# Loading x first and counting, gathering and splitting later in a two-layer graph kernel

## The chip, the cores and the metric

The kernel runs on one core of a Trainium2 chip. The metric is the device time of one execution in microseconds (us). Engines: PE is TensorE, DVE is VectorE, ACT is ScalarE, POOL is GpSimd, SP is SyncE, which here only issues DMAs. ACT issues some as well.

## The reference, cut to what matters

Two layers over 3125 nodes of 256 features and 100000 edges. Each has a graph part, a mixing part and a feed-forward part with experts.

```python
xn = layernorm(x)                                  # x: [3125, 256], no learned scale
neigh = segment_sum(xn[src], dst)                  # 100000 edges, sorted by dst
h = relu(((1 + eps) * xn + neigh) @ W1 + b1) @ W2 + b2
gnn = batchnorm(h)
q, k, v = split(rmsnorm(xn, g_pre) @ w_qkv)        # 4 heads of 32, plus 4 memory keys
q = softmax(q over features) * scale; k = softmax(k over nodes)
mix = rmsnorm((q @ (k.T @ v)) @ w_out + b_out, g_out) + xn
x = x + gnn + mix
x = x + experts0(layernorm(x))                     # top 2 of 8, relu
xn = layernorm(x)
x = x + two_graph_convolutions(xn, edge_weight) + mix1(xn)
xn = layernorm(x)
x = x + gelu(xn @ W1s + b1s) @ W2s + b2s + experts1(xn)   # shared part, and top 2 of 8
```


## The kernel before

X holds 25 tiles of 128 nodes. `first_norm_*` goes over 7 groups of 4 tiles (the last has one). For each, DVE takes statistics (`statistics_dve`) and a variance, ACT the root, DVE the reciprocal and bias, ACT writes the normalised rows XN, PE turns them (`turn_pe`, 8 transposes), ACT and DVE copy a half each to XT (`turn_act`, `turn_dve`), PE makes the q, k, v products of 4 tiles (`first_products_pe`), and ACT evacuates them with a scale (`first_products_act`), two groups behind. A tile's product waits for the evacuation four tiles earlier.

The edges are put to use through windows of two destination nodes. To find where each window begins, the first destination of each of 784 rows of 128 edges (`firsts`) is compared with each window (13 columns of windows: 7 counts on DVE in `windows_dve`, 6 sums of signs on ACT in `windows_act`). With the row numbers GpSimd gathers 13 rows of destinations (`windows_pool`, L306); DVE counts in these (`begins_dve`, L297) and gets where records start; GpSimd gathers 13 lots of records (dst, src, weight; L310). `places_dve` (L331), `places_act`, `places_in_tiles_dve`, `tiles_dve` and `keys_dve` turn records to keys, `good_dve` checks on a total of PE (`total_pe`) that all edges are inside, and `weights_dve` (L318) makes the degrees.

Before, `loads_act` issues the constants, `firsts` and x in three DMAs on ACT's queue, and `early_sp` nine small weights on SP's. All counts stand ahead of the first group. The row gathers run while the groups are normalised; `begins_dve` stands in group 4, and the record gathers follow at once. `mix0_*` is the attention: DVE takes maxima of q and k, subtracts, ACT takes exponentials, PE the context; `q_norm_dve` normalises q; cwo (L949) is the context times w_out; then for 7 groups PE turns q and multiplies, ACT takes squares (L868) and roots (L871), DVE scales (L957 to L967) and adds to X. The order on each engine is written out by hand and kept by semaphores.

SP then stores XN, zero pads (`zero_sp`), loads the late weights (`late_sp`), and stores the mix.

The end of layer 1: `conv_pe` finishes; the last group of 4 tiles is added and normed (`last_*`), while the shared feed-forward part runs over 13 tiles of 256 nodes. `between` orders it: `tile(i)` is the first product of tile i (48 matmuls, L1947), `second(i - 1)` the second product of the tile before (48, L1962), with two steps of routing between (`route_*`; 17 steps on DVE give the slot numbers). A weight is used as a high and a low part: `parts_act` copies the high, `parts_dve` subtracts (L1858). `halves_dve` (L1863, L1865) does so for the input of a tile, `first_dve` (L1886, L1888) for its hidden values. `warm_pe` are small matmuls without use of their result.

PE's order there is: first product of tile 0, 8 warm matmuls, first product of tile 1, the last group's turn, second product of tile 0, scores. ACT does the last group's root ahead of the copy of the second weights and of tile 1; DVE does scales and `parts_dve` ahead of `halves_dve` of tile 1.

## Time and profile before

| | us |
|---|---|
| median of 3 runs | 2214.99 (2212.96 to 2215.39) |
| profiled execution | 2201.3 |
| its span | 2199.7 |
| PE busy | 2063.6 (94%) |
| DVE busy | 1648.3 (75%) |
| ACT busy | 1241.5 (56%) |
| POOL busy | 594.7 (27%) |

The profile's page divides the span in 40 slices of 55 us. PE's busy tenths there start with 5, 7, 6, 9, then are 9 nearly throughout; DVE's start with 6, 9, 9, 8. The clock that the throttle granted to PE is 7 tenths in the third slice, 8 in the twelfth and the last, and 9 in all others. A time in the rows below is counted from the start of the span. A row of the view in order of time may merge several instructions (x4), and then its duration is from the first's start to the last's end.

### The profile page before, as it was taken

The numbers are of one execution on the slowest core, as the hardware profiler recorded it, in microseconds if no ns is written. First come the engines' busy times: TensorE is split into PE (matmuls) and PEld (weight loads), VectorE is DVE, ScalarE is ACT, GpSimd is POOL, SyncE is SP. The second block draws the span as 40 slices with busy tenths as digits, with TensorE's granted clock in tenths as the row PEclk, the third lists the DMA queues.
The fourth block names the chain that finished last, engine by engine and source line by source line (L and its number), as shares of the span: only waits on it lengthen the run. The fifth ranks groups of instructions, "written<-read, shape, count | busy, mean of one in ns | idle before, by whom it ended". The sixth has DMA issues, their size and how long they took to land. (4 is left out here: it accounts for less than half of the span.)

```text
span 2199.7 us, 46493 instructions
## 1 busy us (share of the span) xinstructions
PE 2063.6 (94%) x17860; PEld 1938.7 (88%) x17860; DVE 1648.3 (75%) x3103; ACT 1241.5 (56%) x2885; POOL 594.7 (27%) x462
## 2 busy tenths in 40 slices
PE   5769999999889999998999999999998999999996
PEld 3559999999689999997788999999998999999996
DVE  6998888885688888875657666566656868888885
ACT  6866555554547676665543444444444236767765
POOL 3100000000047777760000000000000016677774
PEclk9979999999989999999999999999999999999998
DMA  4424333344458778774004666466641026787776
GB/s 133 139 91 122 92 105 108 92 116 139 159 173 221 232 223 246 219 232 105 1 26 113 189 188 188 115 179 182 192 147 61 20 95 215 215 243 221 240 223 165
DMA packets 241142, 338.98 MB, mean 154 GB/s; under 512 B 33439, under 2 KB 202578, under 8 KB 240786
## 3 DMA queue, kind: packets, MB, share of 16 engines
q1 hardware_dynamic: 208940, 296.19, 42.5%
q0 software_dynamic: 28528, 35.76, 8.6%
q10 hardware_dynamic: 3446, 3.97, 0.6%
q8 instruction: 146, 2.39, 0.4%
q14 instruction: 82, 0.67, 0.1%
HBM read 258.89 MB, written 76.95 MB: 153 GB/s over the span
## 5 line engine op out<-in xcount | busy, mean ns | idle before, releaser
L2484 PE MATMUL bank<-WB_r,XN_r 128*128 128x448 f32 x1400 | 400.4, 367 | 0.4 <-DVE X L2261 0.4
L2017 POOL DMA_INDIRECT SC<-xd,slot_i x128 | 182.7, 1428 | 791.3 <-DVE slot_q L1653 659.8
L2419 ACT CAST WB_r<-WB 128x448 fp32r<-128x448 f32 x350 | 198.0, 567 | 248.0 <-PE bank L2484 229.3
L2424 DVE TENSOR_TENSOR WB_r<-WB,WB_r 128x448 fp32r<-128x448 f32 x350 | 217.2, 632 | 155.4 <-ACT WB_r L2419 155.0
L2484 PEld LDWEIGHTS bank<-WB_r,XN_r 128*128 128x128 f32 x1400 | 261.2, 188 | 22.6 <-DVE X L2261 0.8
L1947 PE MATMUL bank<-SC_r,WB_r 128*128 128x256 f32 (+1 forms) x2064 | 253.0, 282 | 13.2 <-issue 10.9
L1947 PEld LDWEIGHTS bank<-SC_r,WB_r 128*128 128x128 f32 x2064 | 246.3, 190 | 17.8 <-issue 17.4
L1067 ACT CAST WB_r<-bank 128x200 fp32r<-128x200 f32 x391 | 144.4, 369 | 158.9 <-PE bank L1050 158.2
L1962 PE MATMUL bank<-R_r,H_r 128*128 128x256 f32 x1752 | 215.4, 282 | 5.0 <-DVE R_r L1858 5.0
L1962 PEld LDWEIGHTS bank<-R_r,H_r 128*128 128x128 f32 x1752 | 209.1, 189 | 5.4 <-issue 5.4
L2411 POOL TENSOR_TENSOR WB<-WB,CB 128x128 f32<-128x128 f32 (+1 forms) x56 | 27.3, 488 | 610.9 <-DMA WB<-adjw 609.9
L1947 PE MATMUL bank<-SC_r,XN_r 128*128 128x256 f32 x1392 | 169.4, 280 | 4.2 <-issue 2.9
L1947 PEld LDWEIGHTS bank<-SC_r,XN_r 128*128 128x128 f32 x1392 | 164.6, 188 | 8.1 <-issue 7.7
L1819 ACT ACTIVATE yo<-yo,slot_p 128x256 f32<-128x256 f32 x118 | 53.6, 502 | 208.4 <-DVE yo L1897 203.9
L1810 ACT ACTIVATE wb_<-bank,WB 128x256 f32<-128x256 f32 (+1 forms) x344 | 133.2, 477 | 66.7 <-PE bank L1947 39.1
L2023 POOL DMA_INDIRECT slot_p<-pd,slot_q x128 | 158.8, 1240 | 41.3 <-issue 32.6
L1107 PE MATMUL bank<-H_r,WB_r 128*128 128x256 f32 x625 | 164.9, 299 | 0.0
L2484 PE MATMUL bank<-WB_r,R_r 128*128 128x448 f32 x448 | 164.4, 367 | 0.0
L1107 PE MATMUL bank<-XN_r,WB_r 128*128 128x256 f32 x625 | 153.9, 282 | 0.0
L1067 ACT COPY X<-bank 128x200 f32<-128x200 f32 x391 | 148.5, 380 | 0.0
L1023 DVE TENSOR_TENSOR SC<-R,DR 128x1024 bf16<-128x1024 bf16 x196 | 134.0, 684 | 0.0
L1107 PEld LDWEIGHTS bank<-XN_r,WB_r 128*128 128x128 f32 x625 | 118.7, 190 | 0.1
(480 smaller groups left out, 5118.7 us busy)
## 6 DMA issues: line engine op xcount, KB each, us to landing
WB<-adjw SPq DMA_DIRECT2D x350, 224.0 KB, 2.8
WB<-in_f_pack SPq DMA_DIRECT2D x127, 512.0 KB
WB<-in_f_pack SPq DMA_DIRECT2D x62, 640.0 KB
adjw<-X SPq DMA_DIRECT2D x24, 1600.0 KB, 7.8
WB<-in_f_pack SPq DMA_DIRECT2D x65, 516.0 KB
xd<-XN SPq DMA_DIRECT2D x10, 640.0 KB, 6.7
y<-X SPq DMA_DIRECT2D x10, 640.0 KB, 3.3
X<-y SPq DMA_DIRECT2D x6, 640.0 KB, 7.1
```

The costliest lines, as they stand in the source:

```text
L1023: e.tensor_tensor(by_two(hot_lo[s][:, 0:m, :]), row(iota16, o), along(lo2, o, 128), ALU.is_equal).then_inc(S("lo1"), 1)
L1067: e.copy(to[b % 2][:, :, 8 * j:8 * j + 8].rearrange("p h (q r) -> p q h r", r=2), bank[:, :, i]).then_inc(S(name), 1)
L1107: m = e.matmul(bk[:, 0:D], CNT[b % 2][:, h, :], x[:, h * D:(h + 1) * D], start=(h == 0 and x is xnh), stop=(h == T - 1 and x is xnl), skip ...
L1810: m = e.activation(st[:, q * w:(q + 1) * w], B[hp][:, q * TS:q * TS + w], gfun[L], bias=b[:, hc:hc + 1])
L1819: e.activation(ob[:, q, :], ob[:, q, :], ACT.Copy, scale=slot_p[:, 2 * i + q:2 * i + q + 1]).then_inc(S("obs"), 1)
L1947: m = e.matmul(B[hp][:, q * TS:q * TS + w], p[:, c * HID + hc * 128:c * HID + (hc + 1) * 128], x[:, c * w:(c + 1) * w], start=(c == 0 and ...
L1962: m = e.matmul(bk[:, s * D:(s + 1) * D], x[:, hc * w + s * 128:hc * w + (s + 1) * 128], p[:, hc * D:(hc + 1) * D], start=(hc == 0 and n == ...
L2017: e.indirect_dma_start(yin[i % 2][:, q * D:(q + 1) * D], None, XD, bass.IndirectOffsetOnAxis(ap=slot_i[:, 2 * i + q:2 * i + q + 1], axis=0 ...
L2023: e.indirect_dma_start(slot_p[:, 2 * i + q:2 * i + q + 1], None, PD.rearrange("(r k) -> r k", k=1), bass.IndirectOffsetOnAxis(ap=slot_q[:, ...
L2419: e.copy(split_w(m)[0], RAW[m % PR]).then_inc(S("whigh"), 1)
L2424: e.tensor_tensor(al, RAW[m % PR], ah.bitcast(F32), ALU.subtract).then_inc(S("wlow"), 1)
L2484: mm_ = e.matmul(conv_bank(k, band, c)[:, 0:PW], x[st][:, o], y, start=(st == 0 and i == 0), stop=(st == T - 1 and i == 2))
```

## The change

Loads: SP issues all but the constants, in this order: x tiles 0 to 3, six of the small weights, tiles 4 to 7, tiles 8 to 11, `firsts`, tiles 12 to 23, three weights, the last tile. Groups 0, 1, 2 and 3 wait for their own.

Counts: the cast of `firsts` and the 7 counts of DVE stand in groups 1 to 4 (2, 2, 2, 1), the 6 of ACT in groups 1 to 3 (3, 2, 1), with the row numbers at the end of group 4. `begins_dve` stands behind the last group. GpSimd gathers records only when all first products are made. SP stores XN only when the records are in. Buffers move: `firsts` and its cast to R1, the counts' output to H.

PE makes group 0's products ahead of group 1's turn. In the mix, the places stand on DVE behind all three normalisations of q, then context, shift, low keys, tiles, check, cwo, keys; on ACT behind all of x's sums; on PE behind the context's product.

Shared tiles: PE warms 14 times, the last group's turn stands behind the second product of tile 0, the scores behind that of tile 1; routing steps begin at tile 2; DVE splits the next tile's input straight behind a tile, ahead of the second weights; ACT copies the second weights in tile 0 and does the last group's root and rows behind tile 1.

The diff, with unchanged lines mostly left out:

```diff
 SHT = 13
-W_IN = 16 * 9
+W_IN = 16 * 6
...
     wide_wb = nc.alloc_sbuf_tensor_at("wide_wb", [128, 12000], F32, offset=at["WB"])
-    firsts = WB[:, 0:784].bitcast(I32)
-    firstf = WB[:, 784:1568]
-    below = WB[:, 1568:1568 + WG * 392].bitcast(BF16).rearrange("p (g n) -> p g n", g=WG)
+    firsts = r1_all[:, 1856:2640].bitcast(I32)
+    firstf = r1_all[:, 2640:3424]
+    below = h_all[:, 0:WG * 392].bitcast(BF16).rearrange("p (g n) -> p g n", g=WG)
...
     def loads_act(e):
         e.dma_start(CB[:, :], a["consts"]).then_inc(S("consts"), 16)
-        e.dma_start(firsts, a["first"].partition_broadcast(128)).then_inc(S("first"), 16)
-        for i in range(2):
-            e.dma_start(X[:, 12 * i:12 * i + 12, :],
-                        a["x"][12 * i * 128:12 * (i + 1) * 128, :].rearrange("(t p) d -> p t d", p=128)).then_inc(S(f"x_in{i}"), 16)
-        e.wait_ge(S("set"), 1)
-        e.dma_start(X[0:LAST, T - 1, :], a["x"][(T - 1) * 128:N, :]).then_inc(S("x_in1"), 16)
+
+    def x_tiles_sp(e, t0, t1, name):
+        e.dma_start(X[:, t0:t1, :], a["x"][t0 * 128:t1 * 128, :].rearrange("(t p) d -> p t d", p=128)).then_inc(S(name), 16)
...
     def early_sp(e):
+        x_tiles_sp(e, 0, 4, "x_in0")
...
         e.dma_start(cols[:, 0:16], a["cols"]).then_inc(S("w_in"), 16)
-        e.dma_start(wo0, a["m_wout"]).then_inc(S("w_in"), 16)
-        e.dma_start(bout0, a["m_bout"].partition_broadcast(128)).then_inc(S("w_in"), 16)
-        e.dma_start(gout0, a["m_gout"].partition_broadcast(128)).then_inc(S("w_in"), 16)
...
         e.dma_start(epsc, a["eps"].partition_broadcast(128)).then_inc(S("w_in"), 16)
+        x_tiles_sp(e, 4, 8, "x_re")
+        x_tiles_sp(e, 8, 12, "x_out1")
+        e.dma_start(firsts, a["first"].partition_broadcast(128)).then_inc(S("first"), 16)
+        x_tiles_sp(e, 12, 24, "x_in1")
+        e.dma_start(wo0, a["m_wout"]).then_inc(S("x_in1"), 16)
+        e.dma_start(bout0, a["m_bout"].partition_broadcast(128)).then_inc(S("x_in1"), 16)
+        e.dma_start(gout0, a["m_gout"].partition_broadcast(128)).then_inc(S("x_in1"), 16)
+        e.wait_ge(S("set"), 1)
+        e.dma_start(X[0:LAST, T - 1, :], a["x"][(T - 1) * 128:N, :]).then_inc(S("x_in1"), 16)
...
-    def windows_dve(e, c):
+    COUNTS_DVE = {1: range(0, 2), 2: range(2, 4), 3: range(4, 6), 4: range(6, COUNTED)}
+    COUNTS_ACT = {1: range(COUNTED, 10), 2: range(10, 12), 3: range(12, WG)}
+
+    def firsts_dve(e):
...
         e.wait_ge(S("set"), 5)
-        for g in range(COUNTED):
+
+    def counts_dve(e, c, gs):
+        for g in gs:
             c.add(e.tensor_scalar(below[:, g, :], firstf, w2h[:, g:g + 1], None, ALU.is_lt, ALU.add, accum_out=cnt4[:, g:g + 1]))
+
+    def windows_dve(e, c):
...
         c.add(e.tensor_scalar(row4[:, 0:COUNTED], cnt4[:, 0:COUNTED], 1.0, 0.0, ALU.subtract, ALU.max))
-        e.wait_ge(S("mix0_act"), M0A_PLACES)
+        e.wait_ge(S("mix0_act"), M0A_KEXP)
...
-    def windows_act(e):
-        e.wait_ge(S("consts"), 16)
+    def windows_act(e, gs):
         e.wait_ge(S("set"), 5)
-        for g in range(COUNTED, WG):
+        for g in gs:
...
         e.wait_ge(S("rows"), 2)
+        e.wait_ge(S("qk"), T)
...
+    def shift_dve(e, c):
+        c.add(e.tensor_scalar(whii.bitcast(I32), esrc, 7, None, ALU.logical_shift_right))
+
     def places_in_tiles_dve(e, c):
-        c.add(e.tensor_scalar(whii.bitcast(I32), esrc, 7, None, ALU.logical_shift_right))
...
         def ready(t):
             if t == 0 and k == 1:
-                e.wait_ge(S("x_re"), 80)
+                e.wait_ge(S("x_re"), 96)
...
     M0P_KMAX, M0P_KALL, M0P_CTX, M0P_MASKED, M0P_CWO = range(5)
-    M0A_PLACES, M0A_KEXP, M0A_MEM = WG - COUNTED, WG - COUNTED + 1, WG - COUNTED + 5
-    M0V_W, M0V_RS, M0V_GROW, M0V_REL, M0V_KMAX, M0V_DIAG, M0V_KSUB, M0V_MEM, M0V_MASKED, M0V_CTX, M0V_CWO = (
-        0, 2, 5, 6, 7, 8, 9, 13, 14, 15, 16)
+    M0A_KEXP, M0A_MEM, M0A_PLACES = WG - COUNTED, WG - COUNTED + 4, WG - COUNTED + 5
+    M0V_W, M0V_RS, M0V_GROW, M0V_KMAX, M0V_DIAG, M0V_KSUB, M0V_MEM, M0V_REL, M0V_MASKED, M0V_CTX, M0V_CWO = (
+        0, 2, 5, 6, 7, 8, 12, 13, 14, 15, 16)
...
                 e.wait_ge(S("set"), 4)
+            if g == 1:
+                e.wait_ge(S("x_re"), 16)
+            if g == 2:
+                e.wait_ge(S("x_out1"), 16)
             if g == 3:
-                e.wait_ge(S("x_in1"), 32)
+                e.wait_ge(S("x_in1"), 80)
...
             e.tensor_scalar(sd[:, 0, o], mv[:, o, 1], 1.0, 1e-5, ALU.mult, ALU.add).then_inc(S("var"), 1)
-            if g == 4:
-                begins_dve(e, c)
...
                 turn_dve(e, 0, g - 1)
+            if g == 1:
+                firsts_dve(e)
+            if g in COUNTS_DVE:
+                counts_dve(e, c, COUNTS_DVE[g])
+            if g == 4:
+                windows_dve(e, c)
...
         turn_dve(e, 0, G - 1)
+        begins_dve(e, c)
...
                 first_products_act(e, t)
+            if g in COUNTS_ACT:
+                windows_act(e, COUNTS_ACT[g])
...
     def first_norm_pe(e):
-        for g in range(G):
+        turn_pe(e, 0, 0)
+        first_products_pe(e, 0)
+        turn_pe(e, 0, 1)
+        for g in range(2, G):
             turn_pe(e, 0, g)
-            if g:
-                first_products_pe(e, g - 1)
+            first_products_pe(e, g - 1)
...
         warm_pe(e, 2, 24)
-        total_pe(e)
...
         m.then_inc(S("mix0_pe"), 1)
-        places_pe(e)
...
         e.matmul(B[1][:, 0:D], kb, wo0, start=True, stop=True).then_inc(S("mix0_pe"), 1)
+        places_pe(e)
+        total_pe(e)
...
     def mix0_act(e):
...
         q_exp_act(e, 0)
-        places_act(e)
...
         x_sum_act(e, range(8, T))
+        places_act(e)
...
     def mix0_dve(e, c):
-        places_dve(e, c)
...
         e.tensor_tensor(memkT[:, :], memkT[:, :], kb[0:4, :], ALU.subtract).then_inc(S("mix0_dve"), 1)
-        q_norm_dve(e, c, 0)
-        places_in_tiles_dve(e, c)
-        good_dve(e)
+        for i in range(3):
+            q_norm_dve(e, c, i)
+        places_dve(e, c)
...
         e.scalar_tensor_tensor(km, B[2][:, 0:128], k2[:, 1:2], mask32, ALU.mult, ALU.mult).then_inc(S("mix0_dve"), 1)
-        tiles_dve(e, c)
+        shift_dve(e, c)
...
         e.tensor_copy(kb, B[0][:, 0:128]).then_inc(S("mix0_dve"), 1)
+        places_in_tiles_dve(e, c)
+        tiles_dve(e, c)
+        good_dve(e)
+        e.wait_ge(S("mix0_pe"), M0P_CWO + 1)
+
+        e.scalar_tensor_tensor(cwo, B[1][:, 0:D], HEAD_SCALE, bout0, ALU.mult, ALU.add).then_inc(S("mix0_dve"), 1)
         keys_dve(e, c)
-        e.wait_ge(S("mix0_pe"), M0P_CWO + 1)
-
-        e.scalar_tensor_tensor(cwo, B[1][:, 0:D], HEAD_SCALE, bout0, ALU.mult, ALU.add).then_inc(S("mix0_dve"), 1)
-        q_norm_dve(e, c, 1)
-        q_norm_dve(e, c, 2)
...
             if j == 0 and b == 1:
-                e.wait_ge(S("x_out1"), 32)
+                e.wait_ge(S("x_out1"), 48)
...
             tile(i)
-            if i:
+            if i >= 2:
...
                 second(i - 1)
-            if i:
+            if i >= 2:
...
     def sp_program(e):
...
         e.wait_ge(S("qk"), T)
+        e.wait_ge(S("edges"), 16 * WG)
...
     def act_program(e):
         loads_act(e)
-        windows_act(e)
...
         def begin():
-            e.wait_ge(S("slots"), 3)
+            e.wait_ge(S("slots"), 4)
...
         def tile(i):
+            if i == 2:
+                last_turn_act(e, G - 1)
...
             if i == 0:
+                parts_act(e, 1, 1, SHARED)
+            if i == 1:
                 last_root_act(e, G - 1)
-                parts_act(e, 1, 1, SHARED)
...
                     last_rows_act(e, G - 1, j)
-            if i == 1:
-                last_turn_act(e, G - 1)
...
     def dve_program(e):
...
         sets_dve(e, c)
-        windows_dve(e, c)
...
         def tile(i):
+            if i == 2:
+                last_turn_dve(e, G - 1)
             first_dve(e, 1, NSLOT + i, shared_w(i))
+            if i + 1 < SHT:
+                halves_dve(e, shared_x(i + 1), NSLOT + i + 1, shared_w(i + 1))
             if i == 0:
-                last_scales_dve(e, G - 1)
...
             if i == 1:
-                last_turn_dve(e, G - 1)
-            if i + 1 < SHT:
-                halves_dve(e, shared_x(i + 1), NSLOT + i + 1, shared_w(i + 1))
+                last_scales_dve(e, G - 1)
...
         def tile(i):
...
             if i == 0:
-                warm_pe(e, 6, 8)
+                warm_pe(e, 6, 14)
+
+        def second(i):
             if i == 1:
-                last_turn_pe(e, G - 1)
-
-        def second(i):
+                e.wait_ge(S("xt0"), 4 * G)
...
             if i == 0:
+                last_turn_pe(e, G - 1)
+            if i == 1:
...
```

## Rows read from the trace of the kernel before

**Rows 1.** busy time in two stretches: start:end, length, busy us (instructions), clock, DMA

```profile
20.00:66.00 46.00, 42.00 (x150) 25.73 (x150) 35.88 (x156) 30.57 (x65) 26.09 (x26) 1.00 0.26 75
62.00:106.00 44.00, 28.68 (x178) 24.67 (x177) 40.94 (x111) 38.45 (x64) 0.22 (x1) 0.88 0.52 154
```

**Rows 2.** groups of instructions, 0 to 66 us: busy us, mean ns, idle

```profile
L745 ACT ACTIVATE XN<-X,small 128x256 f32<-128x256 f32 x25 | 13.0, 589 | 4.3 <-DVE small L708 4.3
...
L277 DVE TENSOR_SCALAR_CACHE_REDUCE WB<-WB,CB 128x784 bf16<-128x784 f32 x7 | 6.7, 1023 | 0.0
L291 ACT ACTIVATE WB<-WB,CB 128x784 bf16<-128x784 f32 x6 | 5.6, 935 | 0.0
```

**Rows 3.** VectorE in order of time: start, duration, line, operation, idle before

```profile
19.76 1.41 DVE L495 BATCH_NORM_STATS2 small<-X 128x6 f32<-128x256 f32 x4
...
22.83 0.20 DVE L708 SCALAR_TENSOR_TENSOR small<-small 128x4 f32<-128x4 f32 x1
...
38.77 0.34 DVE L297 TENSOR_SCALAR_CACHE_REDUCE DR<-R,CB 128x128 f32<-128x128 int32 x1
...
62.87 3.04 DVE L331 TENSOR_SCALAR H<-H,CB 128x128 f32<-128x128 int32 x13 [0.47 <-DMA H<-in_edges,small]
65.81 1.61 DVE L886 TENSOR_REDUCE small<-wide_wb 128x44 f32<-128x1408 f32 x1
```

**Rows 4.** busy time and GB/s over the first 9 us

```profile
0.00:5.00 5.00, 0.00 (x0) 0.00 (x0) 2.39 (x7) 0.00 (x0) 0.19 (x4) 1.00 0.54 172
5.00:9.00 4.00, 0.00 (x0) 0.00 (x0) 1.17 (x4) 0.00 (x0) 0.00 (x0) 1.00 0.83 257
```

**Rows 5.** TensorE in order of time, first products to the last

```profile
29.17 1.38 PE L775 MATMUL bank<-wb_,XT 128*128 128x384 f32 x2
...
47.85 0.81 PE L775 MATMUL bank<-wb_,XT 128*128 128x384 f32 x2
...
65.07 0.81 PE L776 MATMUL bank<-wb_,XT 128*128 128x384 f32 x2
```

**Rows 6.** GpSimd in order of time: row gathers, then a record gather

```profile
20.14 1.12 POOL L306 DMA_INDIRECT R<-in_dst,small  x1 [19.39 <-DVE small L285]
...
35.33 0.95 POOL L306 DMA_INDIRECT R<-in_dst,small  x1 [0.30 <-issue]
43.00 0.94 POOL L310 DMA_INDIRECT H<-in_edges,small  x1 [6.73 <-DVE small L301]
```

**Rows 7.** VectorE in order of time, 93 to 110 us

```profile
93.77 0.40 DVE L949 SCALAR_TENSOR_TENSOR yo<-bank,rows 128x256 f32<-128x256 f32 x1
...
105.60 0.16 DVE L957 TENSOR_SCALAR small<-small 128x4 f32<-128x4 f32 x1
...
109.80 0.17 DVE L957 TENSOR_SCALAR small<-small 128x4 f32<-128x4 f32 x1
```

**Rows 8.** ScalarE in order of time, 71 to 108 us

```profile
71.72 1.68 ACT L344 ACTIVATE SC<-R,ones 128x1664 f32<-128x1664 f32 x1
...
107.49 0.21 ACT L871 ACTIVATE small<-small 128x4 f32<-128x4 f32 x1
```

**Rows 9.** TensorE in order of time, first halves of shared tiles 0 and 1

```profile
1658.09 5.84 PE L1947 MATMUL bank<-SC_r,WB_r 128*128 128x256 f32 x48 [0.68 <-issue]
...
1670.82 8.00 PE L1947 MATMUL bank<-SC_r,WB_r 128*128 128x256 f32 x48 [5.10 <-issue]
```

**Rows 10.** busy time and clock over the first half of shared tile 1

```profile
1670.80:1678.70 7.90, 7.88 (x49) 7.90 (x50) 2.53 (x5) 3.81 (x7) 0.00 (x0) 0.70 0.20 67
```

**Rows 11.** VectorE in order of time, near 1666 and 1670 us

```profile
1665.69 0.69 DVE L1888 TENSOR_TENSOR H_r<-wb_,H_r 128x512 fp32r<-128x512 f32 x1
...
1670.03 0.69 DVE L1865 TENSOR_TENSOR SC_r<-XT,SC_r 128x512 fp32r<-128x512 f32 x1
```

**Rows 12.** ScalarE in order of time, near 1665 us

```profile
1664.83 1.28 ACT L2616 ACT_TABLE_LOAD   x1
```

**Rows 13.** GpSimd in order of time, the first gather of the last slots

```profile
1782.69 1.01 POOL L2017 DMA_INDIRECT SC<-xd,slot_i  x1 [145.91 <-DVE slot_q L1653]
```

2 lines of the change are left out of this document (1 added, 1 removed).

## The prediction

> **What bounds the kernel.** I read the busy time by stretch first, because the change touches two places only: the first 110 us and 40 us near 1660. Over 20 to 66 us TensorE is busy 42.0 of 46 us; over 62 to 106 us it is VectorE, 40.9 of 44 us [rows 1]. So the opening has three parts: a wait for x, a TensorE-bound norm with first products, and a VectorE-bound stretch that lasts beyond 106 us. From about 160 us TensorE is full, so what either part saves is still there at the end if nothing later stands at a fixed time. All sums are against the profiled execution (2201.3 us, span 2199.7); the runs' median is 2214.99. I carry the difference over unscaled.
>
> **Part 1, the start.** Before, VectorE counts first rows (7 counts, 6.7 us, so 0.95 each) and ScalarE 6 (5.6 us, 0.93 each) [rows 2] ahead of the first statistics at 19.76; the first group's bias is ready at 23.03, 3.27 us later [rows 3]. Now tiles 0 to 3 are first on SP. With the constants beside them that is 0.88 MB, and 0.86 MB had moved by 5.0 us [rows 4], so I put their landing at 5.3. The first group's scaling of the weights waits for six small loads behind; 1.3 MB, at 257 GB/s from there [rows 4], and small pieces that are issued until about 6 us give 7.7 (ends 7 and 9.5). Bias ready at 9.0: 14.0 us sooner.
>
> The counts aren't gone, only moved. Groups 1 to 4 now carry them: 2, 2, 2, 1 on VectorE with a cast of 0.57, and 3, 2, 1 on ScalarE. ScalarE's round without waits is 4 rows of XN (2.07), a root with its answer from VectorE (0.65), a copy (0.5) and 4 evacuations (2.1), some 5.3 us: 0.589 us for a row [rows 2], less 0.09 where they overlap, and an evacuation taken as long as a row, since both make one tile. TensorE's round is 6.2 us: products of group 0 start at 29.17, of group 3 at 47.85 [rows 5]. So 2.8 and 1.9 us of signs make ScalarE the longer one in groups 1 to 3, and the counts put VectorE's variances late too. Worked through group by group (variance ready, XN written, products start):
> group 0: 7.5, 11.1, 14.7; group 1: 11.2, 14.0, 22.0; group 2: 17.8, 20.6, 29.6; group 3: 25.7, 28.4, 35.8; group 4: 31.1, 34.6, 42.7.
> Group 0's products start 14.5 us sooner, group 3's 12.0, and the last product ends 11.1 us sooner (65.88 becomes 54.8). About 3.4 us of the head start goes back to idle TensorE between groups. The products of group 0 moved ahead of group 1's turn fill some of it; alone they give 0 to 0.6 us.
>
> **Part 2, row and record gathers.** The 13 row gathers are issued every 1.25 us, from 20.14 to 35.33 [rows 6], and the last lands some 2.4 us after its issue, since the counts on these rows could start at 38.77 [rows 3]. That cover was free: before, they ran beside the norm. Now the first can go only when group 4's count is done, 36.6 by the table above, so the last lands at 36.6 + 0.3 + 15.2 + 2.4 = 54.5. VectorE was through with the norm at 62.40, where it waited 0.47 us for the records [rows 3]; now at 62.4 - 11.1 = 51.3, and it stands 3.2 us. The begins take 4.0 us (38.77 to the record gather's start at 43.00, less 0.3 on the queue) and have moved from the norm, where VectorE had room, onto the path: until 58.5. What stood at 65.81, the second group's q maximum [rows 3], starts at 58.8: 7.0 us sooner, not 11.1.
> The new wait of GpSimd for the last product costs nothing, as 54.8 is before 58.5. Records take 62.87 - 43.00 = 19.9 us and are there at 78.5.
>
> **Part 3, VectorE from there to the mix.** From 65.81 to 105.60 [rows 7] it was 39.8 us, the weights at its end included. The same work stands there now in another order, plus the places (2.9 us, 62.87 to 65.81), which were ahead of it; the wait of 1.0 us for the context goes, since three normalisations now stand ahead of it. The records at 78.5 meet VectorE at about 82: no wait. 58.8 + 39.8 + 2.9 - 1.0 = 100.5, and 0.4 for waits on the total, which now comes after the places' turn on TensorE: 100.9, 4.7 us sooner. Next limit: ScalarE's second root ended at 107.70 [rows 8], 2.1 us ahead of VectorE's use at 109.80. Its chain hangs on the first outputs, which start after cwo; cwo (end 94.17 [rows 7]) comes at 58.8 + 28.4 (94.17 - 65.81) + 2.9 for the places + some 5 for two normalisations, now ahead of it (three operations each of at most the 1.61 us at 65.81, the last group's small) - 1.9 for the keys, now behind it - 1.0 = 92.2, and 92.6 with the total's wait. That is 1.6 us sooner, so the root ends at 106.1. VectorE takes it at 106.1 and not at 105.2: 3.7 us sooner. From here both shift together. **Front: -3.7 us**, ends -8 (no stand on rows, root in time) and +2 (weights at 9.5, groups 1 to 4 each 1 us later).
>
> SP stores XN only when the records are in, 78.5 and not 65.9, so its stores of XN, zero fills and late weights slide by 12.6 us. Behind them on SP stand the y stores, the first of which wants the third added pair, some 1.9 us behind 109.80, now 108. Between 65.9 and there SP had 46 us for work of some 8 MB, 27 us at 300 GB/s; it keeps 29. If that doesn't hold, the y stores come late by the rest (0 to 3 us), and the buffers that X's place is to serve with them. The x loads share one queue, constants on the other; group 3 waits for all loads, about 19 us, and comes at 24.
>
> **The Sign activations** now stand between roots. A Sign ran straight behind an Exp's square at 71.72 with no table load in between [rows 8], so it is in the Exp table; whether the sqrt table has it no row shows. I take it that it does. (The Trainium skill, "ScalarE: Activation LUTs", Table sets, says cheap functions are in every set as filler, and names relu, copy, identity and abs; Sign isn't in that list, so it leans my way without settling it.)
>
> **Part 4, the shared tiles.** TensorE's first half of tile 1 started at 1670.82 after 5.1 us of idleness and took 8.00 us; tile 0's took 5.84 [rows 9]. The granted clock over those 7.9 us is 0.70, that is partly the lower level of 1.2 GHz [rows 10]. It waited for the low halves of tile 1, at 1670.03 to 1670.72 on VectorE [rows 11], behind a root with its table load of 1.28 us [rows 12], scales and the second weights' split. Now the halves follow VectorE's split of tile 0, done at 1666.38 [rows 11], directly: 1666.38 + 1.1 = 1667.5. TensorE warms 14 instead of 8 times; 8 took 1.9 us (1663.8 to 1665.7), 14 last until 1663.8 + 3.4 = 1667.2, so the idle gap is 0.3 us and I take the full clock: 1667.5 + 5.84 = 1673.3, against 1678.8. That is 5.4 us. What is late next: the second weights' split ends at 1669.9, used at 1673.4; the root comes after ScalarE's tile 1, at 1674.2 + 1.28 + 0.2 = 1675.7; scales 1676.7; the four rows of XN 1678.9; second half of tile 0 on TensorE ends 1679.2, and the turn of the last group behind it finds them ready by 0.3 us. Halves of tile 2 are there at 1676.3, wanted at 1680. The scores move behind tile 1's second half. I count 0.3 us for a slip: **-5.1 us**, ends -2 and -6.
> Route steps begin a tile later and there are 17, so the slot numbers come in tile 10 and not in 9, 11 us later by tile and some 6 by time. GpSimd took them at 1782.69 [rows 13], needs 13 us for the first two slots' gathers, and TensorE turns the first gathered rows only behind tile 12. Two tiles and more of 11 us lie between; covered by 10 us. The new wait for 4 instead of 3 holds ScalarE's weight copy by 2 us, covered by the product beside it.
>
> **Sum**: -3.7 - 5.1 = -8.8: 2192.5 in a profiled execution like the one before, 2206.2 as median.
>
> **Rivals.**
> A, the front gives nothing (chance 0.20): the gathers and begins, once under the norm, are a chain; each us that group 4's count is later moves all of VectorE. With the weights at 9.5 and four rounds 1 us longer, -3.7 becomes 0 to +2, in sum -4: 2211. For it: VectorE is nearly fully busy behind [rows 1]. Against: 3.2 us of stand are in my sum already.
> B, the Sign is not in the sqrt table (0.10): three groups of signs, two loads each, 6 x 1.28 = 7.7 us on ScalarE, just where it is the longer one; -8.8 + 7.7 = -1.1: 2213.9. The row at 71.72 speaks for a filler.
> By the Trainium skill's "ScalarE: Activation LUTs", What ACT_TABLE_LOAD costs, a switch is 2.66 us with its drain, and B would be +7; the row at 1664.83 shows 1.28, so I price by the row.
> C, the slower side (0.06): TensorE's clock falls in the gaps that now stand between the norm's groups. Products at the lower level take twice 5.16 us a group; two groups lost, and the change is at zero (-8.8 + 10.3); with four, +20.6 less some 4 of gaps: +8, 2223. It decides from the third group. For it: the fall after the idleness at 1665.7 [rows 9, 10]. Against: my gaps are 1 to 3 us, and the stretch to 66 us held full clock [rows 1].
> D, the tile split gives only 2 us (0.10): the clock falls all the same, or the last turn waits for XN: 2209.3.
> E, the whole front in hand (0.04), -8: 2202.
>
> Forecast 0.50. A run here tells 0.2% (4.4 us) from no change. Faster: forecast, E, most of D and half of A: 0.68. Slower: C and a little of A and B: 0.08. Same: 0.24. The range for 8 in 10, with the unknown ends of both parts: 2201 to 2214.
>
> **What would show it.** First XN row near 9 us; products of groups 0, 3 at 14.7 and 35.8; last product near 54.8; no table load in groups 1 to 3; VectorE idle some 3 us before the begins, waiting on the row gather; second q maximum near 58.8; the second normalisation of the mix at 106; in the tail first half of tile 1 with an idle gap under 1 us and 5.84 us long. I am wrong if the second q maximum starts after 63, or if tile 1's first half still takes over 7 us.

## The result, and the profile after

| | us, median (lowest to highest) |
|---|---|
| before | 2214.99 (2212.96 to 2215.39), 3 runs; profiled execution 2201.3, span 2199.7 |
| after | 2199.28 (2197.66 to 2200.47), 3 runs; profiled execution 2199.28, span 2197.7 |
| ratio | 0.9935, 95% interval 0.9919 to 0.9951: 15.7 us less |

Forecast was 2206.2, range 2201 to 2214: the change gave 15.7 us where 8.8 were summed. The two profiled executions differ by only 2.0 us. Both numbers have to be explained.

The same two stretches as in [rows 1], in the kernel after (columns as there):

```profile
20.00:66.00 46.00, 35.28 (x132) 20.91 (x130) 33.65 (x113) 30.33 (x60) 17.26 (x17) 0.96 0.10 28
62.00:106.00 44.00, 27.43 (x159) 25.02 (x160) 41.85 (x111) 34.10 (x58) 15.70 (x15) 0.74 0.68 203
```

TensorE's work has moved ahead of 20 us. Behind 62 us VectorE is as full as before, and TensorE's granted clock is 0.74 instead of 0.88: it is at its lower level of 1.2 GHz for more of the stretch. VectorE in order of time, to be read against [rows 3] and [rows 7]:

```profile
6.12 1.41 DVE L508 BATCH_NORM_STATS2 small<-X 128x6 f32<-128x256 f32 x4 [0.94 <-DMA X<-in_x]
...
9.01 0.16 DVE L723 SCALAR_TENSOR_TENSOR small<-small 128x4 f32<-128x4 f32 x1
...
57.12 0.35 DVE L307 TENSOR_SCALAR_CACHE_REDUCE DR<-R,CB 128x128 f32<-128x128 int32 x1 [2.68 <-DMA R<-in_dst,small]
...
61.12 1.61 DVE L912 TENSOR_REDUCE small<-wide_wb 128x44 f32<-128x1408 f32 x1
...
94.55 0.40 DVE L976 SCALAR_TENSOR_TENSOR yo<-bank,rows 128x256 f32<-128x256 f32 x1
103.22 0.15 DVE L983 TENSOR_SCALAR small<-small 128x4 f32<-128x4 f32 x1
...
109.24 0.17 DVE L983 TENSOR_SCALAR small<-small 128x4 f32<-128x4 f32 x1 [1.75 <-ACT small L897]
```

The reader is to see how a lead melts. The first bias is 13.8 us sooner (9.01 against 22.83), the second maximum of q 4.7 us (61.12 against 65.81), the first group of the mix 2.4 us (103.22 against 105.60) and the second group 0.6 us (109.24 against 109.80), since VectorE waits there for ScalarE's second root. TensorE in order of time, the first products, the key turns and the shared tiles, against [rows 5] and [rows 9]:

```profile
14.70 1.62 PE L801 MATMUL bank<-wb_,XT 128*128 128x384 f32 x2 [2.04 <-ACT XT L563]
16.11 1.49 PE L802 MATMUL bank<-wb_,XT 128*128 128x384 f32 x2
17.39 1.16 PE L801 MATMUL bank<-wb_,XT 128*128 128x384 f32 x2
18.39 0.81 PE L802 MATMUL bank<-wb_,XT 128*128 128x384 f32 x2
...
37.24 0.81 PE L801 MATMUL bank<-wb_,XT 128*128 128x384 f32 x2
...
91.11 3.05 PE L392 MATMUL bank<-CB,H 128*128 128x128 f32 x13 [1.65 <-DVE H L363]
...
1659.95 5.84 PE L1973 MATMUL bank<-SC_r,WB_r 128*128 128x256 f32 x48 [0.87 <-issue]
...
1669.40 5.89 PE L1973 MATMUL bank<-SC_r,WB_r 128*128 128x256 f32 x48 [0.49 <-issue]
```

Tile 1's first half now starts 9.45 us behind tile 0's instead of 12.73 us, and takes 5.89 us instead of 8.00. ScalarE in order of time, the only table load of the norm, and two places at the norm's end:

```profile
1.50 1.28 ACT L764 ACT_TABLE_LOAD   x1 [1.50 <-PEq L2928]
...
14.50 0.95 ACT L301 ACTIVATE H<-R,CB 128x784 bf16<-128x784 f32 x1
...
17.93 0.21 ACT L764 ACTIVATE small<-small 128x8 f32<-128x8 f32 x1 [0.52 <-DVE small L715]
...
51.31 0.58 ACT L781 ACTIVATE wide_wb<-bank,small 128x384 f32<-128x384 f32 x1 [3.67 <-PE bank L802]
...
55.65 0.58 ACT L781 ACTIVATE wide_wb<-bank,small 128x384 f32<-128x384 f32 x1 [1.97 <-PE bank L802]
...
109.00 0.21 ACT L897 ACTIVATE small<-small 128x4 f32<-128x4 f32 x1
```

A Sign (L301) stands between two roots (L764) with no load. And ScalarE was idle for 3.67 us ahead of copying out a product. It is tile 18's (tiles counted from 0, copied in order), and TensorE's row for it, in order of time, ends at 47.35:

```profile
46.54 0.81 PE L802 MATMUL bank<-wb_,XT 128*128 128x384 f32 x2
```

It copied it at 51.31, 4.0 us later. The end of a TensorE row is modelled, so this alone does not say that the product was ready at 47.35. But the trace also records the time of each semaphore update, and TensorE's signal for tile 18, for which ScalarE waits, is there at 51.22, 3.9 us behind the row's end and 0.09 us ahead of the copy. In the profile of the kernel before each of these 25 signals comes within 0.02 us of its row's end. So ScalarE waited for a late signal of TensorE. Late signals of this kind turned out to be the key to most of the missing microseconds.

### The profile page after: what moved, and what is told of

It reads as the page before. It is cut to its first block and busy times, and to the rows that moved or that the text cites. A ratio compares the mean times of both kernels' runs of the same rounds, so it can differ in the third digit from the quotient of the medians.

```text
span 2197.7 us, 46520 instructions
## 1 busy us (share of the span) xinstructions
PE 2071.7 (94%) x17872; PEld 1945.1 (89%) x17872; DVE 1649.9 (75%) x3103; ACT 1240.1 (56%) x2884; POOL 593.8 (27%) x462
```

## Experiments

Five comparisons, each on one chip with its own runs of the kernel before:

| comparison, chip | before, median (lowest to highest), runs |
|---|---|
| 1, A | 2201.53 (2197.93 to 2206.02), 27 |
| 2, B | 2215.43 (2211.36 to 2217.31), 11 |
| 3, A | 2202.12 (2198.71 to 2208.10), 32 |
| 4, C | 2212.27 (2209.26 to 2215.98), 13 |
| 5, D | 2202.32 (2197.65 to 2204.82), 11 |

**The parts, on chip A.** `plain` is the kernel before unchanged, `both` the change whole, `shared_only` and `front_only` the two halves of the diff. The shared half is

```diff
         def tile(i):
+            if i == 2:
+                last_turn_dve(e, G - 1)
             first_dve(e, 1, NSLOT + i, shared_w(i))
+            if i + 1 < SHT:
+                halves_dve(e, shared_x(i + 1), NSLOT + i + 1, shared_w(i + 1))
             if i == 0:
-                last_scales_dve(e, G - 1)
                 parts_dve(e, 1, 1, SHARED)
             if i == 1:
-                last_turn_dve(e, G - 1)
-            if i + 1 < SHT:
-                halves_dve(e, shared_x(i + 1), NSLOT + i + 1, shared_w(i + 1))
+                last_scales_dve(e, G - 1)
...
             if i == 0:
-                warm_pe(e, 6, 8)
...
+                warm_pe(e, 6, 14)
```

with ScalarE's and TensorE's last turn, root and scores moved likewise and the routing steps beginning at tile 2; the front half is everything else.

> The kernel before, unchanged. The profiled execution of before took 2201.3 us and its three timed runs 2213 to 2215.4. Theory S (a spread between loads of one program, of the order of 14 us, that has nothing to do with the change): the timed runs of this copy differ from those of the kernel before, or its profile shows a time more than 5 us away from 2201. Theory R (the 15.7 us are the change's): copy and kernel before agree within 2 us in every round, and the profile of a slow execution shows 14 us more at places that the change touches.

> The changed kernel again. Prediction's sum: 8.8 us less than before. By the two profiles at hand (2201.3 and 2199.3) only 2 us less. By the timed runs 15.7 us less. Theory R: 13 to 18 us less again. Theory S: 3 to 9 us less, with a spread over the rounds as large as the difference.

> Before, with the shared tiles' part of the change alone. Both theories: 5.1 us less (the first half of tile 1 starts 3.3 us sooner and takes 5.84 instead of 8.00 us). If the timed result is over 8 us, the shared part carries something that the profile of the tiles doesn't show.

> Before, with everything of the change but the shared tiles' part. Prediction: 3.7 us less. By the profile of the changed kernel the second root of the mix is taken at 109.2 instead of 109.8 (0.6 us less), 3.7 us of stall near 47 us included. Theory R: 8 to 11 us less, since the shared tiles can give only 5. Theory S: 0 to 4 us less.

| | comparison 1: median, ratio | comparison 3 (again): median, ratio |
|---|---|---|
| plain | 2203.45, 1.0003 (0.9994 to 1.0012) | 2201.61, 0.9998 (0.9989 to 1.0007) |
| both | 2194.31, 0.9962 (0.9948 to 0.9976) | 2195.31, 0.9971 (0.9962 to 0.9981) |
| shared_only | 2196.95, 0.9975 (0.9966 to 0.9984) | 2196.84, 0.9980 (0.9971 to 0.9989) |
| front_only | 2200.68, 0.9991 (0.9982 to 1.0000) | 2200.65, 0.9997 (0.9987 to 1.0006) |

The ratios times 2202 us are: whole change 8.4 and 6.4 us, shared part 5.5 and 4.4, front 2.0 and 0.7. The front's two intervals end at 1.0000 and 1.0006, so on this chip its gain is hardly told from nothing. So on this chip the sum of 8.8 nearly holds, and I took the 15.7 us for three odd runs of the kernel before. Comparison 2 took that away: eleven more runs of it at 2215.43, beside variants of the changed kernel at 2195.6 to 2198.2. What was asked next:

> The kernel before, unchanged, as a kernel of its own with a profile, on whatever chip this comparison gets. So far it stood at 2201.5 (38 runs on one chip), at 2215.4 (11 runs on another, where variants of the changed kernel took 2195.6 to 2198.2) and at 2215.0 in the three first runs. Theory L (two levels of the kernel before, set by the chip): here all its runs lie at one of the two, 2198 to 2206 or 2211 to 2217, with none between; at the upper one its profile shows one place 12 to 15 us longer than in the recorded profile of 2201.3. Theory D (drift spread over the kernel): the profile has each stage longer by its share, 0.6%, with no such place.

> The change without its shared-tile part. At the lower level of the kernel before it was 1 to 2 us faster. If the kernel before is at its upper level here and theory F holds (what costs the 14 us is in the front: x's loads behind others on the queue, or the records), this kernel is at 2198 to 2203, 12 to 16 us under; if theory T holds (it is in the shared tiles or behind them), it is at 2211 to 2215. At the lower level: 2199 to 2202 either way, and nothing is told apart.

> The kernel before with the shared-tile part of the change alone. At the lower level of the kernel before it was 5.5 us faster. If the kernel before is at its upper level here: theory F has this kernel at 2208 to 2212 (its 5.5 us alone), theory T at 2194 to 2199 (5.5 and the 14 us). At the lower level: 2195 to 2198.

> The whole change again. Theory L says that it has no upper level: 2193 to 2200 on every chip, so 7 to 9 us under the kernel before where that is at its lower level and 15 to 19 us where it is at its upper one. If this kernel too has an upper level that it only hadn't met, it may show here at 2207 to 2210.

It got chip A again (table above): nothing told apart, but the parts repeated. Comparison 4 then got a chip on which the kernel before is slow:

> The kernel before, unchanged, with a profile. It stood at 2201.5 and 2202.1 in two comparisons on one chip (59 runs of the reference and 22 of this copy, 2198 to 2208), at 2215.4 in one on another chip (11 runs, 2211 to 2217), and at 2215.0 in the three first runs. If this comparison gets a chip of the upper level, this copy is at 2211 to 2217 and its profile says where: theory F (in the front) has the second maximum of q some 14 us past 66.5, or the second group of the mix some 14 us past 110.5; theory T (in the shared tiles or behind them) has the products of shared tile 0 at their old place and tile 3 past 1698 by 14; theory D (spread over all tiles) has tile 0 of the shared tiles some 10 us past 1658. On a chip of the lower level: 2198 to 2206, every mark within 2 us of these.

> The change without its shared-tile part. Upper level of the kernel before: theory F 2198 to 2203, theory T 2211 to 2215, theory D anywhere between and up to the level of before. Lower level: 2199 to 2202 (0 to 2 us under the kernel before), the second group of the mix near 110.

`plain3` 2212.26 (2207.08 to 2218.41, 10 runs), ratio 1.0000; profiled execution 2210.59. `front_only3` 2201.33 (2197.74 to 2204.02), ratio 0.9949 (0.9932 to 0.9966): the front alone gives 11.3 us there, against 0.7 to 2.0 on chip A. Theory F holds: the difference is in the front. Now VectorE, ScalarE and TensorE of `plain3` in order of time:

```profile
39.76 0.18 DVE L706 RECIPROCAL small<-small 128x4 f32<-128x4 f32 x1 [3.94 <-ACT small L742]
...
59.71 0.16 DVE L706 RECIPROCAL small<-small 128x1 f32<-128x1 f32 x1 [6.32 <-issue]
...
65.35 0.69 DVE L560 COPY XT<-bank 128x512 f32<-128x512 f32 x1 [3.53 <-remote]
...
74.99 1.61 DVE L886 TENSOR_REDUCE small<-wide_wb 128x44 f32<-128x1408 f32 x1
```

```profile
32.87 0.58 ACT L757 ACTIVATE wide_wb<-bank,small 128x384 f32<-128x384 f32 x1 [0.34 <-PE bank L776]
37.80 0.58 ACT L757 ACTIVATE wide_wb<-bank,small 128x384 f32<-128x384 f32 x1 [4.35 <-PE bank L776]
...
59.00 0.58 ACT L757 ACTIVATE wide_wb<-bank,small 128x384 f32<-128x384 f32 x1 [2.97 <-PE bank L776]
...
63.19 0.59 ACT L550 COPY XT<-bank 128x512 f32<-128x512 f32 x1 [2.49 <-PE bank L542]
```

```profile
32.86 0.81 PE L776 MATMUL bank<-wb_,XT 128*128 128x384 f32 x2
...
55.33 1.04 PE L542 MATMUL bank<-CB,XN 128*128 128x128 f32 x8
...
66.19 1.01 PE L775 MATMUL bank<-wb_,XT 128*128 128x384 f32 x2 [4.44 <-ACT wide_wb L757]
66.99 1.49 PE L776 MATMUL bank<-wb_,XT 128*128 128x384 f32 x2
68.27 1.49 PE L775 MATMUL bank<-wb_,XT 128*128 128x384 f32 x2
...
1667.22 5.91 PE L1947 MATMUL bank<-SC_r,WB_r 128*128 128x256 f32 x48 [0.94 <-issue]
```

and the same marks of `plain2`, the same program on chip A:

```profile
37.12 0.18 DVE L706 RECIPROCAL small<-small 128x4 f32<-128x4 f32 x1 [3.04 <-ACT small L742]
...
55.22 0.16 DVE L706 RECIPROCAL small<-small 128x1 f32<-128x1 f32 x1 [4.13 <-ACT small L742]
...
66.91 1.62 DVE L886 TENSOR_REDUCE small<-wide_wb 128x44 f32<-128x1408 f32 x1
```

ScalarE waits 4.35 us in group 0's products: TensorE's row for tile 1's ends at 33.67 (the pair of 32.86, 0.81 long), and the copy is at 37.80. It waits 2.97 us for group 3's last product, and 2.49 us for a turn. The semaphore updates in the trace say what it waited for:

| `plain3`, product of | end of TensorE's row | TensorE's signal | ScalarE's copy |
|---|---|---|---|
| tile 1 | 33.67 | 37.72 | 37.80 |
| tile 15 | 55.49 | 58.91 | 59.00 |
| tile 16 | 57.66 | 65.38 | 65.47 |
| tile 19 | 61.53 | 65.56 | 66.87 |

Every one of ScalarE's waits over 1 us for a product here ends within 0.1 us behind TensorE's signal, so ScalarE does not stand by itself: the signals come late, by up to 7.7 us. The four of tiles 16 to 19 come within 0.2 us of each other, while their rows lie 1.29 us apart. VectorE meets the same: its copy of a turn at 65.35 follows a signal at 65.32, and TensorE's row for that turn (55.33) ends at 56.37. Behind the late signals VectorE also waits for the root that ScalarE issues after the copies, and TensorE for banks, and after TensorE's idle 4.44 us its pairs take 1.49 instead of 0.81 us.

The second maximum of q comes at 74.99 against 65.81 in [rows 3]: 9.2 us, and the distance stays: the first half of shared tile 0 at 1667.22 against 1658.09 [rows 9] is 9.1 us, the span 2209.0 against 2199.7 is 9.3 us. So between these two executions nothing behind the norm differs by these marks. By the medians chip C is 10 us above chip A and chip B 13; the kernel before was not profiled on chip B, and what its rest is stays open. The four executions of the old front on chip A have no idleness over 1.01 us ahead of such a copy, the recorded profile of before none over 0.77, and in all five each signal comes within 0.02 us of its row's end: that is why no row shows it.

ScalarE and VectorE of `front_only3`, on the same chip C:

```profile
50.33 0.58 ACT L781 ACTIVATE wide_wb<-bank,small 128x384 f32<-128x384 f32 x1 [2.09 <-PE bank L802]
53.16 0.58 ACT L781 ACTIVATE wide_wb<-bank,small 128x384 f32<-128x384 f32 x1 [2.25 <-PE bank L802]
```

```profile
58.32 0.35 DVE L307 TENSOR_SCALAR_CACHE_REDUCE DR<-R,CB 128x128 f32<-128x128 int32 x1 [4.01 <-DMA R<-in_dst,small]
```

The waits are there too (2.09 and 2.25 us, where `both2` on chip A shows 0.40 and 0.71 on the same instructions), but VectorE waits 4.01 us for the row gathers anyway, as it does on chip A (4.00 us in `both2`). So the gather chain covers them. It is not the whole of it: ScalarE's waits over 0.9 us for TensorE behind 30 us add up to 14.1 us in `plain3`, 4.3 in `front_only3` and 5.6 in the kernel after, so the new front also meets less of them, and no run tells the two apart. Comparison 5 was to show this for the whole change:

> The whole change beside the kernel before on whatever chip this gets. Theory: the kernel before pays on some chips 7 to 9 us in the first norm, where ScalarE stands 3 to 4.4 us at a time with its product long done and the products stop behind it; in the changed kernel such stands lie beside VectorE's wait for the first rows' gathers. So on such a chip (before at 2210 to 2217): 2195 to 2200, ratio 0.992 to 0.995, stands of 2 to 4 us on ScalarE between 44 and 56, second maximum of q at 61 to 62.7 all the same. On the other kind (before at 2200 to 2203): 2193 to 2196, ratio 0.9955 to 0.9975, no stand of ScalarE over 1 us behind 44. If instead the changed kernel only happened not to meet them, it is at 2205 to 2210 on the first kind.

It got chip D, where the kernel before takes 2202: `both3` 2194.39 (2193.30 to 2196.09), ratio 0.9965 (0.9953 to 0.9978), 7.7 us less, with no such wait. So the whole change was not run beside the kernel before on a chip like B or C again; for those stand the recorded 15.7 us, the front's 11.3 us of comparison 4, and comparison 2 below.

**What bounds the changed front**, on chip B and without the changed kernel beside them:

`warm_start`, in first_norm_pe, around the first turn:

```diff
+        e.wait_ge(S("consts"), 16)
+        warm_pe(e, 7, 18)
...
+        warm_pe(e, 7, 8)
```

`counts_early`, the counts and, in first_norm_dve, behind the variance:

```diff
-    COUNTS_DVE = {1: range(0, 2), 2: range(2, 4), 3: range(4, 6), 4: range(6, COUNTED)}
+    COUNTS_DVE = {1: range(0, 2), 2: range(2, 4), 3: range(4, COUNTED)}
...
+            if g == 4:
+                windows_dve(e, c)
...
-            if g == 4:
-                windows_dve(e, c)
```

`warm_mix`, in mix0_pe, behind the context, the masked turn and the matmul with wo0; `all3` has all three edits:

```diff
+        warm_pe(e, 3, 16)
...
+        warm_pe(e, 3, 8)
...
+        warm_pe(e, 3, 10)
```

> The changed kernel with TensorE's idle front filled: 18 throw-away matmuls ahead of the norm's first turn and 8 behind it, in a bank that is free. In the profile of the changed kernel the first pairs of products took 1.62, 1.49 and 1.16 us, later ones 0.81. Theory 1 (clock at the start): the pairs take 0.81 from the first, group 0's products end 1.7 us sooner, and since groups 1 to 4 follow back to back the last product comes at 54.4 to 55.5 instead of 56 to 57; if the products set the rows and the rows set the begins, the time falls by 1.5 to 1.7 us against the changed kernel (2194.3 on this chip in the last comparison). Theory 2 (rows' chain): the begins wait for the row gathers and these for the counts on VectorE, which don't wait for TensorE, so the last product comes sooner but the second maximum of q stays at 61 to 62.7 and the time within 0.5 us.

> The changed kernel with the last counted windows taken in group 3 of the norm instead of group 4 and the window starts set right behind group 4's variance, ahead of its normalised rows' work. Theory 2 (rows' chain): rows are set some 3 us sooner (34 to 36 instead of 37.4 to 39), the first-row gathers land 3 us sooner, VectorE's wait of 2.7 to 4.0 us ahead of the begins shrinks to under 1, the second maximum of q comes at 58.5 to 60, and the records land 2 to 3 us sooner; the time falls by 1 to 3 us, less what group 4's products lose by the counts taken ahead of them. Theory 3 (clock and second root): what sets the mix is the context's turns and the second root, the sooner records only move the low keys; if TensorE falls to its lower level there again, the time falls by less than 1 us.

> The changed kernel with TensorE kept busy between the context and the key turns: 16 throw-away matmuls behind the context's, 8 behind the masked turn, 10 behind the one for the clip of weights. Before the change these turns took 1.75 us and the q turns 1.0; in the changed kernel 3.05 and 1.95 at the lower clock level, and the second root came 14.05 us behind the clip against 13.5. Theory 3 (clock and second root): the turns are back at 1.75 and 1.0, the second root comes 1.5 to 2.5 us sooner (106.5 to 107.5 instead of 109.0 by the recorded profile), the second group of the mix on VectorE at its first one's end (about 107.4 instead of 109.24), and the time falls by 1 to 2 us. Theory 2: the wait for the second root is covered by what follows, the mix's last group keeps its place, and the time stays within 0.5 us.

> The three edits together. If each theory holds for its own piece, the pieces add, since they lie one behind the other: 1.5 (start) + 1 to 3 (rows) + 1 to 2 (second root) = 3.5 to 6.5 us under the changed kernel, some 2188 to 2191 on a chip where that takes 2194.3. If only one of them sets the end, the gain is that one's alone, 1 to 2 us. It also shows again how the kernel before stands: near 2201 as in the 38 runs of the last comparison and its own profile, or at 2213 to 2215 as in the three first runs.

| | median, ratio to before on chip B | second q maximum | second group of the mix |
|---|---|---|---|
| warm_start | 2195.60, 0.9920 (0.9907 to 0.9933) | 59.73 | 108.63 |
| counts_early | 2198.23, 0.9921 (0.9909 to 0.9933) | 65.32 | 114.25 |
| warm_mix | 2197.32, 0.9922 (0.9909 to 0.9935) | 61.82 | 110.05 |
| all3 | 2197.41, 0.9922 (0.9910 to 0.9935) | 62.23 | 110.84 |

All four are 17 to 18 us under the kernel before by the ratios, and their runs overlap. `all3` was expected 3.5 to 6.5 us under the changed kernel, near 2190, and is no faster than the others. `counts_early` missed: its first row gather started at 36.05 instead of 37.67, but its second q maximum came 4.2 us later than in the kernel after. ScalarE of `counts_early` in order of time:

```profile
48.32 0.58 ACT L781 ACTIVATE wide_wb<-bank,small 128x384 f32<-128x384 f32 x1 [2.95 <-PE bank L802]
...
53.24 0.58 ACT L563 COPY XT<-bank 128x512 f32<-128x512 f32 x1 [3.22 <-remote]
```

Again the waits for late signals, now ahead of the last root and of the turn that the last products need. Here too a signal comes up to 8 us late (row's end 46.80, signal 54.75). TensorE idles 4.67 us and ends its products at 63.9 instead of 57.9, and VectorE starts the begins at 61.33 without a wait for the gathers. So the changed front is not safe from the late signals as such: in this order they are the limit again. In `warm_mix` the key turns take 1.66 us instead of 3.05, and the second root is no sooner (109.81): TensorE, then ScalarE, in order of time:

```profile
92.67 1.66 PE L392 MATMUL bank<-CB,H 128*128 128x128 f32 x13
```

```profile
93.33 2.95 ACT L419 CAST DR<-bank 128x1024 bf16<-128x1024 f32 x4 [1.29 <-PE bank L392]
96.14 1.12 ACT L889 COPY SC<-bank 128x512 f32<-128x512 f32 x2
```

The copies of q's windows wait behind ScalarE's cast of the low keys, 2.95 us at either pace of the turns. That cast follows the low keys on VectorE (L363), 88.62 to 91.06 in the kernel after. Part of the gain is also given back by the edit itself: in `warm_mix` the low keys are done at 91.91, and the turns start at 92.67, behind the throw-away matmuls. From the first root to the second it is 8.5 us in the kernel after (100.46, 109.00) and 8.6 before (98.87, 107.49).

Two were repeated in comparison 5, on chip D beside `both3`:

> The changed kernel with TensorE fed 18 and 8 throw-away matmuls around the norm's first turn, for the first time beside the changed kernel on one chip. Its profile so far: first pairs of products 0.81 instead of 1.62 us, second maximum of q 59.73 instead of 61.1 to 62.7, second group of the mix 108.63 instead of 109.2 to 111.2. Theory 1 (the start's clock is worth what the marks say): 1.3 to 2 us under the changed kernel. Rival (the mix's later waits give it back): within 0.5 us of it.

> The changed kernel with the throw-away matmuls both at the start and around the key turns. Around the key turns alone they brought the turns from 3.04 to 1.66 us, but the second root stood at 109.8 as before them, since ScalarE's cast of the low keys then came ahead of the copies of q's windows. If that holds, this is no faster than with the matmuls at the start alone (within 0.5 us); if the turns' 1.4 us reach the mix, 1 to 1.5 us under it.

`warm_start2` 2193.46 (2191.67 to 2198.06), ratio 0.9964 (0.9952 to 0.9977); `warms`, with both sets of throw-away matmuls, 2194.90 (2191.51 to 2197.14), ratio 0.9965 (0.9953 to 0.9976). TensorE of `warm_start2` in order of time:

```profile
12.56 1.95 PE L589 MATMUL bank<-CB 128*128 128x128 f32 x16
15.12 0.88 PE L804 MATMUL bank<-wb_,XT 128*128 128x384 f32 x2 [0.62 <-issue]
15.85 0.81 PE L805 MATMUL bank<-wb_,XT 128*128 128x384 f32 x2
```

The pairs take 0.81 to 0.88 us from the first, and the second q maximum comes at 59.95 instead of 62.53 in `both3`. But VectorE then waits 2.54 us for the second root and starts the mix's second group at 108.85, and the median is 0.9 us lower with overlapping runs. A part of the lead is lost between the roots: 9.6 us here (98.99, 108.62) against 8.7 in `both3`, where TensorE's eight products between them take 3.62 us against 2.67. In `warms` the low keys are done at 89.79 and the turns start at 91.29, behind the throw-away matmuls, so it is no clean test of the turns. No version was shown to beat the changed kernel.

## Why the prediction was wrong, step by step

**The step that failed** is the first: "All sums are against the profiled execution (2201.3 us, span 2199.7); the runs' median is 2214.99. I carry the difference over unscaled." I saw 13.7 us between the profile and the runs, and no term accounted for it. The execution profiled has no late signal, while the runs lie where chips B and C do (2207 to 2218), and on chip C the norm of the kernel before is 9 us longer by `plain3`. The sum was worked on the one and its result put on the other. Where the kernel before takes 2202, the sum of 8.8 meets 6.4 to 8.4 us; where it takes 2212 the front's term alone is 11.3 us, and where it takes 2215 the whole is 15.7. That the three first runs were on such a chip is inferred: from their level, and from the profile after, which has the late signals (up to 5.4 us). Of the 13 us between the profile and the runs the norm of `plain3` accounts for 9; the other 4 are open. The difference of the two recorded profiles (2.0 us) crosses from one to the other as well, and tells little of the change.

**Part 1, the start** (14.7 for the first products, 54.8 for the end of the last). First products at 14.70, exactly. But group 0's eight pairs took 6.9 us where the prediction counts 5.2 for a group, because its first pairs after TensorE's idleness took 1.62, 1.49 and 1.16 us; the kernel before paid for one pair only, 1.38 [rows 5], and took 5.7 us for its group 0. It shifted group 1 to 23.48 (said 22.0) and group 3 to 37.24 (35.8). The last product ended at 57.90 in the kernel after, 55.7 to 56.9 in the four executions of this front on chip A. `warm_start2` beside `both3` shows the price at the second q maximum, 2.6 us.

**Part 2, gathers.** Rows were set at 37.4 (said 36.6), VectorE stood 2.68 us for the gathers (3.2), 4.00 on chip A. The mechanism is right, but its sizes were short. The begins started at 57.12, not 54.5. Of these 2.6 us 0.8 are the rows; 1.0 is the chain of 13 gathers, which took 16.2 us and not 15.2 from the first's start to the last's, as its tenth was twice as long (GpSimd in order of time):

```profile
47.88 0.95 POOL L316 DMA_INDIRECT R<-in_dst,small  x1 [0.30 <-issue]
49.13 1.99 POOL L316 DMA_INDIRECT R<-in_dst,small  x1 [0.30 <-issue]
...
53.92 0.95 POOL L316 DMA_INDIRECT R<-in_dst,small  x1 [0.30 <-issue]
```

And 0.8 is the last landing, 3.2 us behind its gather's start (57.12 less 53.92) where 2.4 were put. Nor was it seen that this wait would cover waits for late signals, which the kernel before pays in full. "I am wrong if the second q maximum starts after 63": it came at 61.1 to 62.7 in seven executions, between the predicted 58.8 and that bound.

**Part 3, to the mix.** VectorE reached the mix's first group at 103.22 (said 100.9), cwo was done at 94.95 (92.6), the second root at 109.21 (106.1). Of its 3.1 us, 2.3 came with the second q maximum; the rest lies between: the key turns took 3.05 us instead of 1.75 before (TensorE's granted clock over 88 to 96 us is 0.61), and ScalarE's cast of the low keys stands behind them. So this term of the sum was -3.7, and the front measured 0.7 to 2.0 us less by the ratios of `front_only` on chip A. By marks, the second group of the mix starts at 109.8 to 111.8 in the five executions of the old front without late signals (mean 110.7), and at 109.2 to 111.2 in seven of the new one, with and without (mean 110.2).

**The Sign activations.** No load: rival B is excluded. The Trainium skill, "ScalarE: Activation LUTs", Table sets, does not list Sign among the functions that are in every set; here it ran between roots without one, and the trace decides.

**Part 4, the shared tiles.** -5.1, and measured 4.4 to 5.5 us by `shared_only`; in the profiles, first half of tile 0 to that of tile 3 is 34.88 us after (1659.95, 1694.83) and 40.19 before (1658.09, 1698.28): 5.3 us. The granted clock in tile 1's first half is 1.00 instead of 0.70 [rows 10]:

```profile
1669.40:1675.30 5.90, 5.90 (x50) 5.90 (x51) 4.89 (x8) 2.52 (x6) 0.00 (x0) 1.00 0.00 1
```

It started at 1669.40, 1.9 us later than "1667.5", as tile 0 itself was 1.9 us later in this execution.

**The rivals.** A, the front gives nothing, is nearest to what chip A shows: a start that is 14 us sooner is worth 0.7 to 2.0 us there, hardly clear of nothing. C's fall did not come: between the norm's groups the pairs stay at 0.81 to 0.91 us; what there was of it was one slow start and the key turns. E, the whole front in hand, was given 0.04 with the right size for the recorded runs and for another reason. None of the rivals named a cost in the kernel before that its profile does not show.

## What to carry to other kernels

When the profiled execution and the timed runs of the same kernel differ by more than the effect you forecast, that difference is a term of the sum: say which stretch could hold it, and what the change does there. A stretch where several engines hand short work to each other in a tight round suffers from any late signal between them; slack next to it (here a wait for a DMA behind the norm) can cover it, and then the time depends less on the chip even when the best time hardly moves. `counts_early` took that slack away and met the late signals in full. When an engine seems to stand with its input done, look at the time of the semaphore update it waits for before the engine is blamed: the end of a TensorE row is modelled. And a lead at the start should be followed to the last wait ahead of the full stretch: here 13.8 us became 4.7, 2.4 and 0.6.

## What the runs showed of the hardware

One program takes 2202 us on chips A and D and 2212 to 2215 on B and C (70 runs of the kernel before against 24). Chips B, C and D had one comparison each, so that the chip decides it is the likely reading and not a shown one. In the one profile of the kernel before from C the whole 9.3 us lie in 45 us of it, the first norm.

There TensorE's signals for finished products come late. In the recorded profile of before and in the eleven profiles from chips A and D each of the 25 signals comes within 0.02 us of its row's end. In `plain3` they come up to 7.7 us behind it, in the kernel after 5.4, in `warm_mix` 5.4, in `all3` 7.9 and in `counts_early` 8.0. ScalarE's copies start within 0.1 us behind the signal that ends their wait, in both kinds. In four executions of the new front with its counts in place (`after`, `warm_mix`, `warm_start`, `front_only3`) the wait comes ahead of the same instruction, the 70th on ScalarE (3.67, 3.01, 2.98 and 2.09 us), which waits 0.39 or 0.40 us in the executions on A and D. In `counts_early` and `all3` it comes ahead of the 64th (2.95 and 2.57 us). So the place goes with the program.

Why the signals are late was not found, and nothing here tried to take the cause away. The packets of the instruction queues in the profile do not lie at these waits. One thing goes with them: the traces that have late signals also hold fewer semaphore records. Over 40 to 55 us the kernel after keeps 65 and `both2`, the same program on chip A, 233. So the tracing itself may have a part in it, and no run here tells whether an execution without a trace has these waits.

TensorE's first pairs of products after idleness took up to twice their later time although the row of that stretch grants the full clock (kernel after, columns as in [rows 1]):

```profile
14.70:18.40 3.70, 3.70 (x7) 2.05 (x8) 3.32 (x16) 2.92 (x7) 0.00 (x0) 1.00 0.58 189
```

With throw-away matmuls ahead they took 0.81 to 0.88 us. So a granted clock of 1.00 in a row did not mean that the matmuls in it ran at full pace.
